# A third buffer for the outer spectrum in a 32-image convolution, Fourier and feed-forward kernel, two rings cut to pay for it, and a new order of work

## The reference

```python
# layer 0
h = conv7x7_depthwise(x) + conv_b                  # 96 channels
h = layernorm_over_channels(h) * ln_g + ln_b
h = gelu(h @ w1 + b1) @ w2 + b2                    # 96 -> 384 -> 96
x = layer_scale * h + x
# layer 1, on tokens t (3136 tokens of 96 values per image)
a = relu(batchnorm(layernorm(t) @ aw1.T))          # 96 -> 192
X = fft(a, axis=tokens)
X = relu(X.real * r - X.imag * i + rb) + 1j * relu(X.imag * r + X.real * i + ib)
t = t + batchnorm(ifft(X).real @ aw2.T)            # 192 -> 96
f = q(relu(q(q8(layernorm(t)) @ q8(W1).T) + b1))   # 96 -> 384, rounded to 8 and 16 bits
t = t + q(q8(f) @ q8(W2).T + b2)                   # 384 -> 96
```

## Time and profile before

| | |
|---|---|
| Median of 3 runs | 4539.91 us (4538.33 to 4553.29) |
| The profiled execution, its own time | 4545.77 us |
| Span of the profiled execution, first to last instruction | 4544.0 us |
| Mean granted clock of PE | 0.921 of full speed |
| Busy share of the span: PE, DVE, ACT, POOL | 88%, 63%, 54%, 39% |

### The profile page before, as it was taken

The page is one execution under the profiler, slowest core; times in us unless marked ns, Lnnn a source line. Parts: engine busy times, 40 slices in busy tenths (PEclk is TensorE's granted clock), DMA queues, the critical chain, the costliest instruction groups (busy, mean ns, idle before and its releaser), DMA issues.

```text
span 4544.0 us, 82774 instructions
## 1 busy us (share of the span) xinstructions
PE 3990.9 (88%) x21010; PEld 2872.4 (63%) x21010; DVE 2879.7 (63%) x9311; ACT 2468.6 (54%) x5250; POOL 1768.9 (39%) x2437
## 2 busy tenths in 40 slices
PE   5999959888988898999999999999988989899975
PEld 2444436666666666666676667666666666666663
DVE  2333335566766677667777777767766777676764
ACT  2433424455555555556566556655555655565554
POOL 1111163444444444444444444444444444444421
PEclk9999979999999999999999999999999999999986
DMA  6666533444444444434444444444444444444331
GB/s 155 166 174 173 163 96 89 113 116 118 119 110 118 119 118 119 118 109 104 110 110 112 110 116 112 114 111 119 118 116 116 119 113 119 116 118 117 109 92 50
DMA packets 402457, 535.30 MB, mean 118 GB/s; under 512 B 218665, under 2 KB 378905, under 8 KB 382873
## 3 DMA queue, kind: packets, MB, share of 16 engines
q1 hardware_dynamic: 387964, 513.26, 41.7%
q10 hardware_dynamic: 14272, 20.04, 1.8%
HBM read 296.68 MB, written 236.50 MB: 117 GB/s over the span
## 4 chain that ended last, share of the span: by engine, by line
PE 53%; DMA 15%; DVE 4%; issue 4%; ACT 3%; SPq 3%; POOL 3%; POOLq 0%; DVEq 0%; ACTq 0%
PE psum L1019 10%; PE psum L1013 7%; PE psum L1053 6%; DMA outer_spectrum<-outer 5%; PE psum L1033 5%; PE psum L1041 5%; DMA inner_inverse<-unmixed 4%; DMA inner<-outer_spectrum 4%; PE psum L1082 3%; PE psum L1064 3%; PE psum L1075 3%; PE psum L1103 3%; PE psum L1110 2%; ACT xn L829 2%; POOL scales L707 2%
## 5 line engine op out<-in xcount | busy, mean ns | idle before, releaser
L707 POOL TENSOR_TENSOR scales<-sums,minus_half 112x4 f32<-112x4 f32 (+1 forms) x480 | 658.4, 1372 | 1010.7 <-DVE sums L874 1010.7
L753 POOL TENSOR_TENSOR both<-plus,minus 128x224 f32<-128x224 f32 (+2 forms) x768 | 487.9, 656 | 1140.4 <-DVE minus L932 915.7
L1013 PE MATMUL psum<-hn,w_sb 96*128 96x448 f32 x1344 | 594.3, 582 | 1.6 <-ACT hn L774 1.6
L1019 PE MATMUL psum<-hid,w_sb 128*96 128x448 f32 x1344 | 577.7, 568 | 9.0 <-ACT hid L789 8.9
L789 ACT ACTIVATE hid<-psum,b_sb 128x448 f32<-128x448 f32 x672 | 416.4, 631 | 304.8 <-PE psum L1013 271.9
L932 DVE SCALAR_TENSOR_TENSOR plus<-psum,spec,uw 128x224 f32<-128x224 f32 (+2 forms) x768 | 325.0, 423 | 310.4 <-ACT uw L807 307.4
L401 PE MATMUL c_psum<-c_xt,c_toeplitz 128*112 128x448 f32 x1152 | 476.3, 551 | 48.3 <-ACT c_xt L343 24.4
L724 POOL TENSOR_SCALAR h_norm<-h,sums,scales 112x96 f32<-112x96 f32 x896 | 463.6, 534 | 69.7 <-PE psum L1006 69.4
L807 ACT ACTIVATE uw<-psum,spec 128x224 f32<-128x224 f32 (+2 forms) x768 | 361.2, 525 | 237.8 <-PE psum L1053 237.8
L1053 PE MATMUL psum<-inner_dft,inner 112*128 112x112 f32 x2816 | 419.9, 298 | 74.5 <-DMA inner<-outer_spectrum 74.5
L1053 PEld LDWEIGHTS psum<-inner_dft,inner 112*128 112x128 f32 x2816 | 396.4, 213 | 131.4 <-issue 113.6
(11 more groups left out here) (97 smaller groups left out, 7245.8 us busy)
## 6 DMA issues: line engine op xcount, KB each, us to landing
outer_spectrum<-outer SPq DMA_DIRECT2D x224, 336.0 KB
inner<-outer_spectrum SPq DMA_DIRECT2D x32, 1764.0 KB, 11.3
c_xpad<-x SPq DMA_DIRECT2D x96, 392.0 KB, 11.3
h_tokens<-c_h SPq DMA_DIRECT2D x24, 1568.0 KB, 8.3
h<-h_tokens SPq DMA_DIRECT2D x32, 1176.0 KB, 17.9
x_sb<-x SPq DMA_DIRECT2D x32, 1176.0 KB, 7.6
residual_stream<-t SPq DMA_DIRECT2D x224, 168.0 KB, 2.5
inner_inverse<-unmixed SPq DMA_DIRECT2D x224, 168.0 KB, 2.3
```

The costliest lines, as they stand in the source:

```text
L707: nc.gpsimd.tensor_tensor(scales[which][:, at:at + w], su[:, :, 5], minus_half[:, 0:w], ALU.pow).then_inc(ready.sem, 1)
L753: last = nc.gpsimd.tensor_tensor(both[:, g % 2, kind, 0:w, k * PT // 2:(k + 1) * PT // 2], half(plus), half(minus), ALU.subtract if k else ...
L1013: pe.matmul(bank("M1", c, m, CW, 128), w1_sb[:, m * 128:(m + 1) * 128], hn[:, c * CW:(c + 1) * CW], start=True, stop=True).then_inc(m1_mad ...
L1019: last = pe.matmul(dst, w2_sb[:, m, :], hid[:, c % 2, m, :], start=(m == 0), stop=(m == KF - 1))
```

## The change

Three things are changed. `outer` gets a third buffer, so ACT's copy of A c waits for the store of A c - 3. To make room, `h_norm` goes from four buffers to three, `y16` from two to one, and the matrix that centres `aw1` once, before the loop, is made in `hn` instead of in a tensor of its own. And nearly all numbers of `STAGES` and `LATER` are others (two lines of it are shown), so the lists of all five engines are in another order.

```diff
 STAGES = {
-    2: {"B": (0.5, 4.3, KINDS * NG), "W": (16.5, 9.7, ND), "IB": (28.0, 8.9, ND)},
...
+    2: {"B": (7.0, 3.8, KINDS * NG), "W": (21.0, 9.3, ND), "IB": (26.5, 8.9, ND)},
...
-    "sp": {"M2": 20.5, "IB": 12.0, "A": 15.0, "FETCH": -12.0, "FETCH NEXT": 3.0},
+    "sp": {"M2": 14.0, "IB": 18.0, "A": 8.5, "FETCH": 7.0, "FETCH NEXT": -1.5},
 }
...
@@ -475,13 +475,13 @@
-        h_norm = sb("h_norm", [PT, 4, CH, C])
+        h_norm = sb("h_norm", [PT, 3, CH, C])
...
-        outer = sb("outer", [ROWS, 2, CH, H2])
+        outer = sb("outer", [ROWS, 3, CH, H2])
...
-        y16 = sb("y16", [C, 2, CW], F16)
+        y16 = sb("y16", [C, CW], F16)
...
-        outer_stored = [signal(f"outer_stored{n}", 4 - n, 32) for n in range(2)]
+        outer_stored = [signal(f"outer_stored{n}", len(range(n, NC, 3)), 32) for n in range(3)]
...
-        constant_rows(nc, wts, inner, back, act1, psum)
+        constant_rows(nc, wts, inner, back, act1, hn[:, 0:C], psum)
...
-                            sp.dma_start(g_dram[CH * c:CH * c + CH, rows, :].rearrange("q m h -> m q h"), outer[rows, c % 2, :, :]
-                                         ).then_inc(outer_stored[c % 2].sem, 16)
+                            sp.dma_start(g_dram[CH * c:CH * c + CH, rows, :].rearrange("q m h -> m q h"), outer[rows, c % 3, :, :]
+                                         ).then_inc(outer_stored[c % 3].sem, 16)
...
-                        b, j = before(n + 1, c, NC, 4)
+                        b, j = before(n + 1, c, NC, 3)
                         pool.wait_ge(ht_made.sem, ht_made.at(b, j))
...
-                                h_norm[:, c % 4, j, :].rearrange("p (k c) -> p k c", c=CC), h[:, :, q, :],
+                                h_norm[:, c % 3, j, :].rearrange("p (k c) -> p k c", c=CC), h[:, :, q, :],
...
                     if name == "A":
-                        b, j = before(n, c, NC, 2)
-
-                        act.wait_ge(outer_stored[c % 2].sem, outer_stored[c % 2].at(b, j // 2))
+                        b, j = before(n, c, NC, 3)
+
+                        act.wait_ge(outer_stored[c % 3].sem, outer_stored[c % 3].at(b, j // 3))
                         for m in range(2):
                             act.wait_ge(outer_made.sem, outer_made.at(n, 2 * c + m))
-                            nc.scalar.copy(outer[:, c % 2, 2 * m:2 * m + 2, :].rearrange("p t h -> p (t h)"),
+                            nc.scalar.copy(outer[:, c % 3, 2 * m:2 * m + 2, :].rearrange("p t h -> p (t h)"),
                                            bank("A", c, m, 2 * H2, ROWS)).then_inc(outer_done.sem, 1)
...
-                        act.wait_ge(result_done.sem, result_done.at(*before(n, c, NC, 2)))
-                        nc.scalar.copy(y16[:, c % 2, :], bank("F2", c, 0, CW, C)).then_inc(y16_done.sem, 1)
+                        act.wait_ge(result_done.sem, result_done.at(*before(n, c, NC, 1)))
+                        nc.scalar.copy(y16[:, :], bank("F2", c, 0, CW, C)).then_inc(y16_done.sem, 1)
...
-                        v = y16[:, c % 2, :]
+                        v = y16[:, :]
...
-def constant_rows(nc, wts, inner, back, act1, psum):
+def constant_rows(nc, wts, inner, back, act1, centre, psum):
...
+            nc.vector.tensor_scalar(centre, wts.ident[0:C, 0:C], 1.0 / C, None, ALU.subtract).then_inc(centred, 1)
...
-            dve.wait_ge(centred, 1)
+            dve.wait_ge(centred, 2)
...
         @block.tensor
         def _(pe):
-            pe.matmul(psum[0:C, 0, 0:H2], wts.centre[:, :], wts.aw1[:, :], start=True, stop=True).then_inc(centred, 1)
+            pe.wait_ge(centred, 1)
+            pe.matmul(psum[0:C, 0, 0:H2], centre, wts.aw1[:, :], start=True, stop=True).then_inc(centred, 1)
...
-        self.centre = sb("centre", [C, C])
...
-    nc.vector.tensor_scalar(wts.centre[:, :], wts.centre[:, :], 1.0 / C, None, ALU.subtract)
```

More of the change, by code:

```diff
@@ L94 @@
 STAGES = {
-    1: {"M1": (0.0, 11.9, NC), "M2": (5.0, 11.5, NC), "T": (14.0, 11.8, NC), "W1": (23.0, 11.5, NC),
-        "A": (32.5, 11.9, NC)},
-    2: {"B": (0.5, 4.3, KINDS * NG), "W": (16.5, 9.7, ND), "IB": (28.0, 8.9, ND)},
-    3: {"AP": (-5.0, 11.5, NC), "S2": (8.0, 10.6, NC), "N2": (17.0, 11.0, NC), "T2": (17.5, 11.0, NC),
-        "F1": (18.5, 11.7, NC), "G": (20.5, 10.3, NC), "F2": (33.5, 11.4, NC)},
-    "next": {"L0S": (35.5, 6.2, NC), "L0N": (127.5, 2.9, NC), "HT": (102.0, 2.1, NC)},
-    "fetch": {"FETCH": (-18.5, 10.5, NC - 3)},
-    "fetch next": {"FETCH NEXT": (95.0, 3.8, 3)},
+    1: {"M1": (0.0, 11.9, NC), "M2": (6.5, 11.5, NC), "T": (13.5, 11.6, NC), "W1": (23.5, 11.6, NC),
+        "A": (27.0, 11.9, NC)},
+    2: {"B": (7.0, 3.8, KINDS * NG), "W": (21.0, 9.3, ND), "IB": (26.5, 8.9, ND)},
+    3: {"AP": (-3.5, 11.7, NC), "S2": (5.5, 10.6, NC), "N2": (7.5, 11.2, NC), "T2": (18.0, 11.3, NC),
+        "F1": (22.0, 11.1, NC), "G": (29.0, 11.8, NC), "F2": (39.5, 11.8, NC)},
+    "next": {"L0S": (46.0, 5.7, NC), "L0N": (126.5, 3.4, NC), "HT": (121.0, 1.5, NC)},
+    "fetch": {"FETCH": (7.5, 10.7, NC - 3)},
+    "fetch next": {"FETCH NEXT": (73.0, 2.7, 3)},
 }
 LATER = {
[4 rows of a table removed]
[4 rows of a table added]
     "pe": {},
@@ L1005, in turn @@
                             at = CH - 1 - (CH // 2 * (j % 2) + j // 2)
-                            last = pe.transpose(dst[:, at * PT:(at + 1) * PT], h_norm[:, c % 4, j, :],
+                            last = pe.transpose(dst[:, at * PT:(at + 1) * PT], h_norm[:, c % 3, j, :],
                                                 ident[0:PT, 0:PT])
@@ L1233, in weight_loads @@
         (wts.w1[:, :], w1), (wts.w2[:, :, :], w2.rearrange("(k p) c -> p k c", p=128)),
-        (wts.centre[:, :], ident_c[0:C, 0:C]), (wts.b2[:, :], col(b2, C)), (raw.scale_column[:, :], col(layer_scale, C)),
+        (wts.b2[:, :], col(b2, C)), (raw.scale_column[:, :], col(layer_scale, C)),
         (wts.aw1[:, :], aw1),
```

## The result

The changed kernel took **4285.61 us** (median of 4 runs, 4281.72 to 4286.86) against 4542.61 us (4 runs, 4538.33 to 4553.29) for the kernel before, timed beside it. The ratio is 0.9429, with a 95% interval from 0.9411 to 0.9448: 257 us less, or 8.6 us at each of the 30 turn boundaries. The forecast was 4423 us, the range 4321 to 4520.

A forecast was written before the change was run, and what follows sets the result against it. The prediction took PE to bound the kernel, with a hole at every turn boundary. The boundary would go from 38.6 to 34.7 us, 3.9 less at each of 30, 117 us in all: 4423 us, range 4321 to 4520.

The forecast's parts named there:

- The three waits named: PE's waits at the turn boundary for `back`, `hn` and `inner`, together 9.3 us a turn in the kernel before.
- Landings are in turn: On the transfer queue: each transfer lands behind those issued before it; moving the x load saves 4.1 us on the last inner store.
- The rival by which the move is worth nothing: On the queue: landings not in turn, AP 0 stays at 25.2 us, gain 0.7 a turn, 4519 us; chance 0.08.
- POOL paces AP 0: At the boundary: HT 0 begins at 13.6 us, four POOL chunks take 7.1, AP 0 starts at 22.0 instead of 25.2.
- The ring of three: Three h_norm buffers at HT: L0N 3 waits for HT 0; as rival, gain only 0.8 us a turn, 4516 us, chance 0.08.
- One row of `y16`: ACT's copies at the boundary: costed at nothing under POOL's chain; without that cover 1.0 us, 31 us in all.
- the account: Sum at the turn boundary: 38.6 us before, 34.7 after, a gain of 3.9 us a turn.
- AP 0 to the end of M2 0: Boundary's second part on PE: 9.9 us at the low clock, with M1 0 at 4.4 and M2 0 at 3.0.
- The rival of the full clock: Behind HT: PE's small pieces keep the clock up, gain 7.3 us a turn, 4321 us; chance 0.10.
- Together 38.6: Old boundary at 2130 us: 25.2 us from M2 6's end to AP 0, another 13.4 to the end of M2 0.
- The rest of the turn: Outside the boundary: PE idles under 2 us, the new order has the same work; costed at nothing.
- The rival on the slower side: First half of the turn: PE waits for DVE, losing 7 us a turn, 4633 us; chance 0.10.

The follow-up runs named there:

- x_late: Changed kernel with the x load issued right ahead of IB 7's store instead of behind M2 6's: 4412.98 us, ratio 0.9741.
- x_early: Kernel before with one number of SP's table changed, so M2 6's store and the x load go out ahead of IB 6's store: 4391.32 us, ratio 0.9684.
- the two `split` kernels: h_norm chunks 5 and 6 moved from POOL to DVE: in the changed kernel 4224.62 us, ratio 0.93; in order_only 4183.48 us, ratio 0.9223.
- order_only: Kernel before with the changed kernel's table but its own buffers (two outer, four h_norm, two y16 rows): 4279.80 us, ratio 0.944.
- rings_only: Changed kernel's buffers with the table of the kernel before: 4535.20 us, ratio 0.9996.
- warm2: Changed kernel plus eight matmuls a turn with unused results on PE, ahead of the HT steps' wait for h_norm: 4237.27 us, ratio 0.9355.
- x_b: Kernel before with x_early's one number, and steps B and W laid later so B 0 comes behind M2 0: 4400.63 us, ratio 0.9693.

## Why the prediction was wrong

What held, step by step:

- **The boundary is the place.** The three waits named are gone, ACT's wait for the outer store too.
- **Landings are in turn**, that is, in the order of issue. AP 0 was forecast without `back` in its way; `x_late` and `x_early` show the x load's place to be worth 127 to 143 us in either kernel. The rival by which the move is worth nothing is refuted: a small store behind a large load of the same queue took 7.8 us and 1.9 without it, and of 51 transfers that SP issued while a load of x was under way, between 1500 and 3450 us of the trace of before, none landed ahead of that load. The Trainium skill's page "DMA: Bandwidth & Descriptors", section "Queues, rings and completion order", does say that completion is not in order per issuing engine, but I drew too much from it. Its case is a later transfer on one DMA engine beside an earlier one on sixteen. It also says that a semaphore increment lands only after every earlier write from the same DMA engine. By that a store that shares its DMA engines with the load ahead of it would wait for the load, and the trace agrees (7.8 us against 1.9).
- **POOL paces AP 0.** HT 0 at 13.6 us and AP 0 at 22.3, against 13.6 and 22.0. That is what the four waits in HT and the two `split` kernels show.
- **The ring of three** delays AP 0 (by 0.9 us against `order_only`), as the sum had it. That it costs time was wrong: the clock gives it back, 4285.61 against 4279.80 us.
- **One row of `y16` costs nothing** in the new order, where POOL's chain covers it; in `rings_only`, under the old order, PE waited for it 10.2 us in 15 turns.

What failed is the account: 3.9 us a turn forecast, 8.6 measured. AP 0 came 0.3 later than forecast. Against that, the sum had three terms wrong:

1. *AP 0 to the end of M2 0*, "I take the low clock here as before": 9.9 forecast, 8.1 measured. M1 0 takes 3.40 us, not 4.4, and M2 0 2.50, not 3.0, because the low stretch is 6.8 us long and ends in the middle of M1 0. **1.8 us.** The rival of the full clock was about half true; `warm2` shows what was left of it.
2. *The baseline.* "Together 38.6" was read at one boundary. The boundary one turn earlier shows the spread:

```profile
2000.10 2.42 PE L1019 MATMUL psum<-hid,w_sb 128*96 128x448 f32 x6
...
2044.02 0.93 PE L1082 MATMUL psum<-outer_inv,back 115*96 115x112 f32 x8
```

   That is 41.5 us from the end of M2 6 (2002.52) to AP 1. The one at 2235 us gives 39.6, those at 2352 and 2471 us 40.9 and 41.3, by the same two rows. The mean over all steady boundaries is 40.2 to the end of M2 0 (the 38.6 ended where AP 1 starts, 0.2 earlier). **1.6 us**, and the trace could have told it: the wait for `inner` was 1.50 us at my boundary, where the earlier trace rows has 35.7 us for 16, a mean of 2.2.
3. *"The rest of the turn"*, costed at nothing. It was worth a gain. Before, the turn outside the boundary took 117.8 (the mean of all steady turns) less 40.2, or 77.6; after, 109.2 less 30.45, or 78.8, of which the forecast had 2.8 for B 0, B 1 and the A step that moved in, less S2 0 that moved out. That leaves 76.0: **1.6 us.** The windows of this part of one turn, before and after, say what it is made of:

```profile
2044.30:2121.70 77.40, 76.45 (x452) 57.12 (x451) 68.47 (x244) 51.33 (x114) 32.47 (x41) 1.00 0.26 67
```

```profile
2066.00:2144.80 78.80, 78.80 (x474) 59.99 (x472) 68.64 (x242) 55.58 (x123) 32.86 (x45) 1.00 0.35 94
```

   PE idled 0.95 us there and now not at all; T2's wait for ACT's `xn` (L1095), 10.3 us in 16 turns or 0.65 a turn, was the larger part of it. I had written that PE idles for under 2 us in the rest, which was right, and then put the new order's effect on it at zero. And the steps that moved in cost less than I had them: PE is busy for 78.8 us against 76.6 (means of the steady turns), 2.2 more where I had 2.8.

The sum is 3.9 − 0.3 + 1.8 + 1.6 + 1.6 = 8.6. The range took in a better clock, but not the other two with it, and its low end was the full clock by itself.

The rival on the slower side, a wait for DVE in the first half, did not come. That it was no idle fear `x_b` shows, where the same move of B without the rest of the table brought new waits for ACT of 2.9 us a turn.

The x load's place and SP's list (145 us) are shown, and so is that the rest (about 110 us) comes with the order of the four engines. How these 110 us divide among the table's numbers stays open.

## What to carry to other kernels

On a queue that is served in turn, look at what was issued just ahead of the small store on which a hand-over hangs. A large load there holds the store for as long as it runs itself (7.8 us against 1.9 here), and moving it up by one place can be worth more than a buffer: here 143 us for one number and nothing for the buffer. When a change shortens a repeated hole, measure the hole over many repeats, not at one, and count what the lower clock costs in and behind it, for a shorter hole also gives back clock. Before a buffer is paid for, ask what would end the wait once it is there.
